# GpSimd issues the stores of the split down weights and the reloads of the raw ones, instead of SyncE

## What is computed

```python
g = einsum('bsd,edf->ebsf', h, Wg);  u = einsum('bsd,edf->ebsf', h, Wu)
expert_outs = einsum('ebsf,efd->ebsd', silu(g) * u, Wd)
x = x + (1 - sg) * einsum('be,ebsd->bsd', gating, expert_outs) + sg * shared
...
scores = tanh(x @ W1 + b1) @ v
p = softmax(where(mask, scores, -1e30))
x = x + (p @ x) / cnt
```

## Time and profile before

| | before |
|---|---|
| median of 3 runs | 1127.67 us (1126.43 to 1129.34) |
| the profiled execution, its device time | 1127.99 us |
| the profiled execution, its span | 1126.1 us |
| granted TensorE clock, mean | 0.995 |
| PE busy | 1104.9 us, 98% |
| DVE busy | 919.6 us, 82% |
| ACT busy | 709.4 us, 63% |
| POOL busy | 696.5 us, 62% |
| transfers | 241.24 MB, 214 GB/s in the mean |

### The profile page before, as it was taken

One profiled execution on the slowest core, in us unless ns is written; L12 is line 12 of the kernel. 1 busy time (PEld: TensorE's weight loads), 2 busy tenths in 40 slices (PEclk: granted clock), 3 DMA queues, 4 the chain that ended last, 5 costly groups with the idle time before them and its releaser, 6 DMA issues. The chain is left out here.

```text
span 1126.1 us, 16076 instructions
## 1 busy us (share of the span) xinstructions
PE 1104.9 (98%) x4856; PEld 903.9 (80%) x4856; DVE 919.6 (82%) x1218; ACT 709.4 (63%) x1268; POOL 696.5 (62%) x666
## 2 busy tenths in 40 slices
PE   8799999999999999999999999999999999999988
PEld 6577888778888888888878887888888888888866
DVE  6698777788877877787668899888888898888875
ACT  6475666566666666666556666666666666666663
POOL 7799999999987777778324444444444444444451
PEclk9899999999999999999999999999999999999999
DMA  6666665487666666666545555555555555555512
GB/s 218 251 259 233 249 231 212 177 306 283 235 259 262 261 237 235 239 233 255 218 173 203 179 198 182 203 204 203 206 206 206 206 206 205 206 205 206 203 41 75
DMA packets 66484, 241.24 MB, mean 214 GB/s; under 512 B 6496, under 2 KB 38752, under 8 KB 57184
## 3 DMA queue, kind: packets, MB, share of 16 engines
q1 hardware_dynamic: 65584, 239.70, 57.6%
q10 hardware_dynamic: 816, 0.52, 0.2%
HBM read 134.29 MB, written 105.91 MB: 213 GB/s over the span
## 5 line engine op out<-in xcount | busy, mean ns | idle before, releaser
L811 ACT ACTIVATE silu<-g_ps 128x512 f32<-128x512 f32 x144 | 86.3, 599 | 180.1 <-PE g_ps L1480 180.1
L1478 PE MATMUL v_both<-xs_hi,wq 128*128 128x512 f32 x432 | 170.0, 393 | 3.3 <-DVE up L1146 2.6
L1479 PE MATMUL v_both<-xs_hi,wq 128*128 128x512 f32 x432 | 168.6, 390 | 0.0
L1480 PE MATMUL v_both<-xs_lo,wq 128*128 128x512 f32 x432 | 168.5, 390 | 0.0
L1141 DVE TENSOR_TENSOR gate<-e_ps,v_part 128x512 f32<-128x512 f32 x144 | 99.0, 687 | 66.4 <-PE e_ps L1480 66.2
L805 ACT ACTIVATE v_both<-g_ps 128x512 f32<-128x512 f32 x144 | 83.9, 583 | 101.7 <-PE g_ps L1480 101.4
L711 POOL TENSOR_TENSOR a<-a,a_own 128x512 f32<-128x512 f32 x35 | 56.1, 1604 | 137.4 <-DVE a_own L1173 137.4
L708 POOL TENSOR_TENSOR s<-a_own,a 128x512 f32<-128x512 f32 x35 | 56.3, 1610 | 131.0 <-DVE a_own L1192 131.0
L1478 PE MATMUL g_ps<-xs_hi,wq 128*128 128x512 f32 x288 | 113.0, 392 | 9.5 <-ACT v_both L805 9.5
L817 ACT ACTIVATE p_sb<-e_ps 128x512 f32<-128x512 f32 x144 | 86.2, 598 | 48.4 <-PE e_ps L1480 47.5
L1478 PE MATMUL e_ps<-xs_hi,wq 128*128 128x512 f32 x288 | 112.7, 391 | 0.4 <-ACT p_sb L817 0.4
(11 more groups left out here) (233 smaller groups left out, 2883.5 us busy)
## 6 DMA issues: line engine op xcount, KB each, us to landing
wq_kept<-wq SPq DMA_DIRECT2D x72, 896.0 KB, 5.5
wq<-wq_kept SPq DMA_DIRECT2D x72, 896.0 KB, 4.5
wd_kept<-wd SPq DMA_DIRECT2D x36, 1024.0 KB, 5.4
wd<-wd_kept SPq DMA_DIRECT2D x36, 1024.0 KB, 6.1
raw_d<-in_L_cond_Wd SPq DMA_DIRECT2D x32, 256.0 KB, 3.1
raw<-in_L_cond_Wg SPq DMA_DIRECT2D x31, 256.0 KB, 2.7
raw<-in_L_cond_Wu SPq DMA_DIRECT2D x31, 256.0 KB, 3.5
out_x<-x SPq DMA_DIRECT2D x8, 256.0 KB, 2.1
```

Source lines behind the costliest of these rows:

```text
L811: nc.scalar.activation(silu0[:, i % 2, :], g_ps[:], ACT.Silu).then_inc(silu0_done, 1)
L1478: nc.tensor.matmul(ps, w_hi, a_hi, start=start, stop=False, skip_group_check=True)
L1479: nc.tensor.matmul(ps, w_lo, a_hi, start=False, stop=False, skip_group_check=True)
L1480: return nc.tensor.matmul(ps, w_hi, a_lo, start=False, stop=stop, skip_group_check=True)
```

## The change

SyncE no longer issues the load of raw down weights for pairs 2 to 35 nor the stores of `wd`, and no longer waits for `td_split`. GpSimd issues both from its own queue in a new function `keep_d(k)`, called right behind `sums_d(k)`. The reloads count on new semaphores `restaged_d`, for which `split_d` waits from pair 2 on. The two first loads (pairs 0 and 1) stay on SyncE. No computation is changed.

```diff
@@ SyncE
-                if n % PAIR == PAIR - 1:
-                    k = n // PAIR
-                    sp.wait_ge(td_split, k + 1)
-                    if m < NU // PAIR:
-                        load_d(sp, m)
-                    sp.dma_start(wd_kept[k], wd[:, k % DR].bitcast(F32)).then_inc(wd_stored[k % DR], 16)
@@ GpSimd
             def split_d(n):
                 s, j = n // PAIR % RAWS, n % PAIR
-                if j == 0:
-                    pool.wait_ge(staged_d[s], (n // PAIR // RAWS + 1) * 16)
+                if j == 0 and n // PAIR < RAWS:
+                    pool.wait_ge(staged_d[s], 16)
+                elif j == 0:
+                    pool.wait_ge(restaged_d[s], n // PAIR // RAWS * 16)
...
+            def keep_d(k):
+
+                pool.wait_ge(td_split, k + 1)
+                if k + RAWS < NU // PAIR:
+                    load_d(nc.gpsimd, k + RAWS, restaged_d)
+                nc.gpsimd.dma_start(wd_kept[k], wd[:, k % DR].bitcast(F32)).then_inc(wd_stored[k % DR], 16)
...
                 if n == 3:
                     sums_d(0)
+                    keep_d(0)
                 if n % PAIR and n > 1:
                     sums_d(n // PAIR)
+                    keep_d(n // PAIR)
```

More of the change, by code:

```diff
@@ L276, in cond_resid_kernel @@
         staged_d = [sem(f"staged_d{s}") for s in range(RAWS)]
+        restaged_d = [sem(f"restaged_d{s}") for s in range(RAWS)]
         wq_stored = [sem(f"wq_stored{s}") for s in range(WR)]
@@ L446, in load_gu, with load_d @@
             load_w(queue, m, u, range(PAIR), slice(0, 4, 3), staged_u[m % RAWS])
-        def load_d(queue, m):
+        def load_d(queue, m, sems):
             e, f = uses[m * PAIR]
@@ L451, in load_d @@
             queue.dma_start(raw_d[:, m % RAWS, 0:PAIR * KD, :].rearrange("p (j k) d -> p j (k d)", k=KD),
-                            d[f * P:(f + PAIR) * P, :].rearrange("(j p) d -> p j d", p=P)).then_inc(staged_d[m % RAWS], 16)
+                            d[f * P:(f + PAIR) * P, :].rearrange("(j p) d -> p j d", p=P)).then_inc(sems[m % RAWS], 16)
         def load_x(queue, b, i):
@@ L470, in _ @@
             sp.dma_start(sg[:], shared_gate.unsqueeze(0).broadcast_to([P, B])).then_inc(gates_loaded, 16)
-            load_d(sp, 0)
+            load_d(sp, 0, staged_d)
             for i in range(NJ // PIECE):
                 load_x(sp, 1, i)
-            load_d(sp, 1)
+            load_d(sp, 1, staged_d)
             sp.dma_start(ptype_i[:], prompt_type.unsqueeze(0).broadcast_to([P, B])).then_inc(l1_loaded, 16)
```

## The result

| | before | after |
|---|---|---|
| median, 4 runs each | 1128.20 us (1126.43 to 1129.34) | 1145.61 us (1143.78 to 1145.83) |
| the profiled execution, its device time | 1127.99 us | 1145.7 us |
| the profiled execution, its span | 1126.1 us | 1144.0 us |
| granted TensorE clock, mean | 0.995 | 0.990 |

A forecast was written before the change was run, and what follows sets the result against it. GpSimd, with no margin at pair 14, was taken as the bound: -5.0 + 13 x 2.2 = 23.6 us, plus 2.1 us of slow clock, is +25.7 us, so 1153.7 us, or 1153.4 by the median; range 1136 to 1189.

The forecast's parts named there:

- The bound and its place: GpSimd's combines bound the kernel from pair 3 on; lateness at pair 14 counts for all, 23.6 us.
- the zero margin at `round_w(28)`: Pair 14's combine ends at 223.65 and ScalarE's rounding of block 28 starts at 223.69: nothing to spare.
- X: GpSimd's added time a pair: one reload issue, one store issue and the wait for L587 ahead of them; 2.2 us.
- The slope: Thirteen blocks of issues stand ahead of combine 14, all counted as lateness: 13 x 2.2 us.
- The gain of 5.0 us: Early, ahead of combine 3: GpSimd's 4.99 us wait disappears once loads no longer stand behind SyncE's wait; -5.0 us.
- The slow clock, 2.1 us: TensorE runs at the 1.2 GHz level after the last gap near the masks; 2.1 us, once.
- Nothing for VectorE: The sum held no term for VectorE being slowed by GpSimd's issues; 0 us.
- The later point, combine 35: Last pair of the first half: 34 issue blocks cost 18 us there, below 23.6; equal at 2.5 us a block.
- Rival 1: A dear issue on GpSimd, stretched beside VectorE or by rows: 3 to 4 us a pair, +45 to +79 us; 21%.
- Rival 2: A cheap issue on GpSimd, as on SyncE's free queue: 0.84 to 1.5 us a pair, 1136 to 1145 us; 15%.
- Rivals 3: GpSimd's issues run beside its sums, near 0 us a pair: -5.0 us, 1123 us; 4%.
- 4: No difference: GpSimd's issues cost 0.13 to 0.65 us a pair, time stays within 3.4 us; 3%.

The follow-up runs named there:

- experiment 4: Kernel 1 plus four GpSimd memsets of 128x256 behind each pair's sums, no transfer on GpSimd: 1143.69 us, ratio 1.0130.
- experiment 8: Constants, flags and masks made behind the first half's last sums: from the changed kernel 1124.10 us (0.9964), from kernel 1 1120.97 us (0.9934).
- experiment 5: Changed kernel with each pair's two issues moved behind the next combine in GpSimd's queue, pair 0's left in place: 1139.78 us, ratio 1.0102.
- kernel 1: The kernel before with both transfers left on SyncE but issued one pair later, nothing added to GpSimd: 1125.46 us, ratio 0.9985.
- experiment 2: Kernel 1 with the stores alone issued by GpSimd, the reloads left on SyncE: 1133.40 us, ratio 1.0049.
- experiment 3: Kernel 1 with the reloads alone issued by GpSimd, the stores left on SyncE: 1134.43 us, ratio 1.0058.
- experiment 6: Changed kernel with each pair's store cut into two of 512 KB, three issues a pair on GpSimd: 1148.85 us, ratio 1.0186.
- experiment 1: The run that made kernel 1: from the kernel before, SyncE issues both transfers one pair later: 1125.46 us against 1127.16, ratio 0.9985.

## Why the prediction was right, and where its numbers were off

- **The bound and its place: right.** No view of the share of busy time said it; the zero margin at `round_w(28)` did. The waits stand where they were expected (pair 3, then behind each piece of extra work), the longest near the masks, the 10 us wait is gone, and experiments 4 and 8 show both halves of it: time on GpSimd without transfers costs the same, transfers with room for GpSimd cost little.
- **X, the term that was mis-sized: 2.2 us forecast, 1.63 measured.** The step was the middle between SyncE's 0.84 and twice L587's 3.4. The measured issues are 0.76 and 0.56 us, each well below the 1.3 us that SyncE takes under load and longer than SyncE's with a free queue. They hardly vary: the 34 reloads took 0.741 to 0.958 us, the 36 stores 0.555 to 0.583. Nearest would have been the free row (0.84) and a fixed part. The other part of the step, 0.1 us of wait for L587's end, was too small: 0.30 us stand ahead of every first issue, and experiment 5 shows that it isn't that wait.
- **The slope, 13 us of lateness for each us of X: too steep.** Over kernel 1, combine 14 came later by 7.35, 9.5, 16.2, 16.6 and 21.9 us for 11.7, 13.8, 20.3, 21.2 and 28.0 us of held time (experiments 2, 3, 4, the change, 6): between six and eight tenths. The reason that the trace gives is in GpSimd's own sums: from combine 3 to combine 14 its instructions without the issues took 158.1 us, against 163.6 before, and the combine's first sum 1.30 us in the mean in place of 1.66. They could run faster because VectorE has less to do while TensorE stands still, or because a combine behind an issue never meets a remainder already running. Two experiments speak for the first as the larger part. In experiment 5 no combine from pair 3 on stands behind an issue, and the instructions still took 158.9 us. In experiment 8 the issues stand ahead of the combines, but GpSimd is not late in this stretch: 135.8 us with them, 137.0 with SyncE issuing, 1.2 us less where it is 4.9 between kernel 1 (163.0) and the changed one. That VectorE is what slows them stays argued.
- **The gain of 5.0 us: too large.** It is 3.8 us at combine 3 and 1.7 us in time (experiment 1). The end of pair 1's sums was read from a stretch in which VectorE was idle because of the very gap that the change removes.
- **The slow clock, 2.1 us: right**, 2.1 by the count of matmuls, 2.7 by the starts of blocks 28 and 40.
- **Nothing for VectorE: wrong** by 1.6 us, the long remainders that begin within an issue.
- With X = 1.63 the sum of the forecast is -5.0 + 21.2 + 2.1 = 18.3, close to the 17.4 measured, and that is partly luck: the slope is 4 us too large at combine 14, and the VectorE term (1.6), the rest of the slow clock (0.6) and 1.3 us near the end are missing. The last are a low clock in the profiled execution that the change is not shown to cause.
- **The later point, combine 35, was not reached**, as the forecast had it for X below 2.5. A steady pair takes GpSimd 14.1 to 14.4 us, below TensorE's 15.0.
- **The rivals.** Rival 1 needed X of 3 to 4, and issues that stretch beside VectorE; they don't. Rival 2 is the nearest in its time (1145 at its upper end) and in its ground, SyncE's rows, though 1.63 lies just beyond its 1.5. Rivals 3 and 4 fall with the first row of an issue: GpSimd computes nothing while it issues.

The port rule that I had named for rival 1 (the Trainium skill, "SBUF — State Buffer", Who interferes with whom) has a second half: a VectorE instruction with two SBUF inputs contends with a GpSimd instruction that reads SBUF. The trace agrees with that half: the remainder that began within an issue lasted 2.75 us while the combine behind it took its shortest 1.30. The Trainium skill says in the same section that the order of issue decides who blocks. That does not fit this place as it stands: the remainder began at 358.99, 0.49 us before the combine, and it was the remainder that was held up; whether the issue ahead of the combine is the reason no run shows. What it says of GpSimd being kept from writing descriptors no row here shows, and the estimate of 2.0 us for X from the Trainium skill's "DMA: Bandwidth & Descriptors" was 0.4 us above the measured 1.63.

## What to carry to other kernels

On GpSimd a transfer's issue takes the engine's time like a compute instruction: count it at its held time, 0.6 to 0.8 us here plus 0.3 us for the first, times the number of issues up to the point where GpSimd's lead is smallest, and expect somewhat less (six to eight tenths of it came through here). Look for that point by comparing when an engine ends a piece with when the piece is wanted, at several places, not by its busy share. If a queue is blocked by a wait, first try to issue the same transfers later on that queue (1.7 us faster here), and look for work with no deadline that stands ahead of work with one (about 5 us more for moving constants and masks, and 2 to 3 for the order of two sums).

## What the runs showed of the hardware that I had not expected

- An issue holds GpSimd for 0.56 us for a store of 1024 KB and 0.55 us for one of 512 KB, 0.74 to 0.76 us for a reload of 256 KB, and 0.30 us of idle time stand ahead of the first of a row of issues, whether or not it has to wait.
- VectorE's two-input sum over SBUF, 1.08 us as a rule and 1.94 at most before, took 2.43 to 2.98 us in five of the seven places of the changed kernel where it began within an issue of GpSimd; in each of the five the combine behind the issue began while it ran, and it ended 0.96 us after the combine's first sum. With memsets in the issue's place the longest took 2.13, with the issue behind the combine 1.98.
- GpSimd's issue to landing took 5.7 us in the median for the stores and 3.4 for the reloads, against 5.4 and 3.1 by SyncE.
